# Cross attention: the maximum's scores in three units of one PSUM bank, and projections between the second and third pair of turned scores, in two banks

## What is computed

```python
q_c = _ln(x) @ W_qc + b_qc
kv_c = _ln(context) @ W_kvc + b_kvc
k_c, v_c = jnp.split(kv_c, 2, axis=-1)
...
c_attn_w = jax.nn.softmax(jnp.einsum('bhqd,bhsd->bhqs', q_c, k_c) * scale, axis=-1)
c_attn_out = jnp.einsum('bhqs,bhsd->bhqd', c_attn_w, v_c)
```

## Time and profile before

| | us |
|---|---|
| median of 3 runs (2774.58 to 2776.41) | 2776.03 |
| span of the profiled execution | 2771.8 |
| self-attention, about | 780 |
| cross-attention, about | 1230 |
| of it, one full body in the steady part | 74.45 |

### The profile page before, as it was taken

One profiled execution on the slowest core, in us unless ns is written; L12 is line 12 of the kernel. 1 busy time (PEld: TensorE's weight loads), 2 busy tenths in 40 slices (PEclk: granted clock), 3 DMA queues, 4 the chain that ended last, 5 costly groups with the idle time before them and its releaser, 6 DMA issues. The chain is left out here.

```text
span 2771.8 us, 50094 instructions
## 1 busy us (share of the span) xinstructions
PE 2667.6 (96%) x18676; PEld 2153.0 (78%) x18676; DVE 1743.5 (63%) x3285; ACT 1118.3 (40%) x2187; POOL 1296.9 (47%) x1447
## 2 busy tenths in 40 slices
PE   8999999999789999999999999999889999999997
PEld 6788888887677778777877877777568888888886
DVE  6777777777636777777777766776754444444431
ACT  4344444444434555555545555554532212112110
POOL 2344545444414676776676676666811220220211
PEclk9999999999899999999999999999789999999999
DMA  8454453545252443444344434433431111111110
GB/s 225 125 129 122 124 138 106 130 121 144 91 136 77 110 110 105 106 109 115 105 108 117 108 103 117 109 80 96 126 110 39 36 52 35 42 46 35 42 42 23
DMA packets 169359, 269.86 MB, mean 97 GB/s; under 512 B 28928, under 2 KB 83200, under 8 KB 169104
## 3 DMA queue, kind: packets, MB, share of 16 engines
q1 hardware_dynamic: 166048, 259.33, 34.5%
q0 software_dynamic: 3072, 7.34, 0.8%
HBM read 111.11 MB, written 36.77 MB: 53 GB/s over the span
## 5 line engine op out<-in xcount | busy, mean ns | idle before, releaser
L1490 DVE TENSOR_REDUCE cross_nmax<-cross_sc_ps 112x1 f32<-112x750 f32 x512 | 459.6, 928 | 162.7 <-PE cross_sc_ps L1365 162.6
L1608 ACT ACTIVATE cross_prT<-cross_tr_ps 125x448 f32<-125x448 f32 x768 | 389.9, 544 | 153.5 <-PE cross_tr_ps L1384 146.2
L1655 POOL TENSOR_TENSOR cross_part<-cross_prT 125x448 f32<-125x448 f32 x252 | 290.9, 1154 | 149.4 <-PE cross_or_ps L1404 83.4
L1017 POOL TENSOR_TENSOR self_psum<-self_prT 112x224 f32<-112x224 f32 x256 | 173.3, 677 | 349.4 <-ACT self_prT L907 337.0
L1384 PE MATMUL cross_tr_ps<-cross_qst,cross_kst 98*125 98x224 f32 x1536 | 314.4, 291 | 8.5 <-ACT cross_prT L1608 3.9
L1384 PEld LDWEIGHTS cross_tr_ps<-cross_qst,cross_kst 98*125 98x125 f32 x1536 | 244.6, 190 | 92.8 <-ACT cross_prT L1608 39.2
L1657 POOL TENSOR_TENSOR cross_part<-cross_part,cross_prT 125x448 f32<-125x448 f32 x252 | 291.9, 1158 | 19.8
L2052 ACT ACTIVATE mlp_hv<-mlp_h_ps,mlp_b 128x512 f32<-128x512 f32 x112 | 77.1, 689 | 519.8 <-PE mlp_h_ps L73 505.7
L1365 PE MATMUL cross_sc_ps<-cross_kst,cross_qst 96*112 96x500 f32 (+1 forms) x1024 | 274.2, 350 | 5.5 <-DVE cross_nmax L1490 2.3
L1969 DVE CAST mlp_hT_h<-mlp_hv 128x512 fp32r<-128x512 f32 x112 | 53.5, 477 | 319.1 <-ACT mlp_hv L2052 319.1
L907 ACT ACTIVATE self_prT<-self_st_ps 112x448 f32<-112x448 f32 x256 | 139.1, 544 | 210.6 <-PE self_st_ps L487 210.5
(11 more groups left out here) (247 smaller groups left out, 6644.9 us busy)
## 6 DMA issues: line engine op xcount, KB each, us to landing
cross_kst<-cross_nat_h SPq DMA_DIRECT2D x512, 93.8 KB, 2.2
cross_c_in<-in_context SPq DMA_DIRECT2D x96, 250.0 KB
cross_kst<-cross_nat_l SPq DMA_DIRECT2D x256, 93.8 KB, 2.2
cross_qst<-qc SPq DMA_DIRECT2D x192, 112.0 KB, 2.4
self_kst<-self_nat_h SPq DMA_DIRECT2D x128, 112.0 KB, 2.3
self_qst<-self_natq_h SPq DMA_DIRECT2D x128, 112.0 KB, 3.1
self_x_in<-in_x SPq DMA_DIRECT2D x16, 448.0 KB, 3.8
self_kst<-self_nat_l SPq DMA_DIRECT2D x64, 112.0 KB, 2.3
```

Source lines behind the costliest of these rows:

```text
L1017: pool.tensor_tensor(psum[:, j], prT[:, j, 0], prT[:, j, 1], ALU.add).then_inc(p_summed, 1)
L1490: dve.tensor_reduce(nmax[:, g % 2, t, j:j + 1], sc_ps[t][0:QN, SC0:SC0 + S], AX_X, ALU.max, negate=True).then_inc(maxed, 1)
L1608: act.activation(prT[:, slot(h), 2 * c:2 * c + 2], bank((h + LAG) % NH, c)[0:SN, 0:2 * N].rearrange("p (k t) -> p k t", k=2), ACT.Exp).the ...
L1655: pool.tensor_tensor(part[:], prT[:, j, 0:2], prT[:, j, 2:4], ALU.add).then_inc(pre_summed, 1)
```

## The change

The maximum's scores go into three units of one bank each (`UNITS`): 500 keys of the first half of the queries, 500 of the second, and the last 250 keys of both. Three reductions write `parts`, and one more instruction on DVE takes the smaller of the two negated maxima (`m_least`). Fills use two banks in turn, `even_ps` and `odd_ps`, by their place in `ORDER`, c tiles included, so the two banks `tr_ps` serve the turned scores alone. The maxima of four heads are turned in one transpose of 16 columns into `even_ps` or `odd_ps`, copied once and stored by two DMAs. The fill now stands between the second and the third pair of turned scores. `FILL` has its steps without a projection at 6 and 15, and step 15 has two c tiles.

```diff
-        sc_ps = [ps(f"sc_ps{i}", (P, 1024)) for i in range(QT)]
+        sc_ps = [ps(f"sc_ps{u}") for u in range(3)]
+        even_ps = ps("even_ps")
...
-        pj_ps = ps("pj_ps")
+        odd_ps = ps("odd_ps")
...
+        UNITS = (((0, 0, SHALF[0], 0),), ((1, 0, SHALF[0], 0),), ((0, SHALF[0], SHALF[1], 0), (1, SHALF[0], SHALF[1], SHALF[1])))
...
-        FILL = [[("k", 0, 0)], [("k", 0, 1)], [("k", 1, 0)], [("k", 1, 1)], [], [("k", 2, 0)], [("k", 2, 1)], [], [("v", 0)], [("k", 3, 0)], [("k", 3, 1), ("c", 0)], [("v", 1), ("c", 1)], [("v", 2), ("c", 2)], [("v", 3), ("c", 3)], [("v", 4), ("c", 4)], [("v", 5), ("c", 5)]]
+        FILL = [[("k", 0, 0)], [("k", 0, 1)], [("k", 1, 0)], [("k", 1, 1)], [("k", 2, 0)], [("k", 2, 1)], [], [("v", 0)],
+                [("k", 3, 0)], [("v", 1)], [("k", 3, 1)], [("v", 2), ("c", 0)], [("v", 3), ("c", 1)], [("v", 4), ("c", 2)],
+                [("v", 5), ("c", 3)], [("c", 4), ("c", 5)]]
...
+        TURN_BANK = (0, 1, 1, 0)
...
+        def bank_free(b, fill):
+
+            i = ORDER.index(fill)
+            return latest(b, i % 2, i)
...
         def bank(h, c):
-            return tr_ps[(3 * h + c + sum(len(tile_at(i)) for i in range(h))) % 2]
+            return tr_ps[(h + c) % 2]
...
-            def fill_(body_b, fill):
+            def fill_(body_b, fill, halves=(0, 1)):
...
+                if 0 in halves and body_b.c >= 0:
                     wait(pe, *bank_free(body_b, fill))
+                    wait(pe, m_row, body_b.n(KC, turns_before(fill)))
...
-            def score(b, h, t):
+            def score(b, h, u):
...
-                wait(pe, maxed, b.n(NH * QT, h * QT + t - 1))
+                wait(pe, maxed, b.n(NH * 3, h * 3 + u - 2))
...
-                wait(pe, exped, b.n(3 * NH, 3 * h + (1 if c == 2 else 0 if before or c == 1 else -1)))
+                wait(pe, exped, b.n(3 * NH, 3 * h + c - 1))
...
             def body(b, att, nxt, prv):
                 a = b.plus(1)
                 for h in range(NH):
-                    for c in range(ST // 2):
-                        for f, o in fill_at(b, h, "kv") if c == 1 else ():
-                            fill_(o, f)
...
+                    for o, l in late(b, h, att, prv):
+                        score_t(o, l, 0)
+                    for o, l in late(b, h, att, prv):
+                        score_t(o, l, 1)
+                    if h < NH - 1 and att:
+                        score(b, h + 1, 0)
...
+                    for f, o in fill_at(b, h, "kv"):
+                        fill_(o, f)
+                    if h % HPG == HPG - 1 and att:
+                        turn_maxima(b, h // HPG)
+                    for o, l in late(b, h, att, prv):
+                        score_t(o, l, 2)
+                    for u in (1, 2):
+                        if h < NH - 1 and att:
+                            score(b, h + 1, u)
...
             def split_maxima(b, g):
+                dve.wait_ge(maxed, b.n(NH * 3, 3 * HPG * (g + 1)))
+                dve.tensor_tensor(nmax[:, g % 2], parts[:, g % 2, 0], parts[:, g % 2, 1], ALU.min).then_inc(m_least, 1)
+                dve.wait_ge(m_least, b.n(KC, g + 1))
...
@@ block.scalar, body
-                        for f, o in fill_at(b, h, "kv") if c == 1 else ():
+                        for f, o in fill_at(b, h, "kv") if c == 2 else ():
                             high(o, f)
```

More of the change, by code:

```diff
@@ L1170, in fill_at, with evicted, latest, turns_before @@
             return [(f, b) for f in FILL[h] if f[0] in kinds and exists(b, f[0])]
[L1172 to L1177, removed]
+        def evicted(b, fill):
+            kind, *where = fill
+            o = b.plus(OF[kind])
             if kind == "k":
                 return k_l, o.n(2 * KC, 2 * where[0] + where[1] + 1)
-            return v_done, o.n(ST, where[0] + 1)
+            return {"v": v_done, "c": cT_l}[kind], o.n(ST, where[0] + 1)
+        TURN_BANK = (0, 1, 1, 0)
+        def latest(b, parity, count):
+            mine = [(b.plus(-1), f) for f in ORDER[parity::2] if b.c > 0 and exists(b.plus(-1), f[0])]
+            mine += [(b, f) for f in ORDER[:count][parity::2] if exists(b, f[0])]
+            return evicted(*mine[-1]) if mine else (v_done, ST)
+        def bank_free(b, fill):
+            i = ORDER.index(fill)
+            return latest(b, i % 2, i)
+        def turns_before(fill):
+            step = [h for h in range(NH) if fill in FILL[h]][0]
+            return (step + 1) // HPG if fill[0] == "c" else step // HPG
+        def turn_bank_free(b, g):
+            step = HPG * g + HPG - 1
+            return latest(b, TURN_BANK[g], sum(len(FILL[h]) for h in range(step)) + len([f for f in FILL[step] if f[0] != "c"]))
         def place(b, fill):
-            return pj_ps if b.c >= 0 else FIRST_BANKS[FIRST.index(fill) % len(FIRST_BANKS)]
-        def turn_bank(b, t):
-            return tr_ps[t % 2] if b.c < -1 else tr_ps[1]
+            if b.c >= 0:
+                return (even_ps, odd_ps)[ORDER.index(fill) % 2]
+            return tr_ps[fill[1] % 2] if fill[0] == "c" else FIRST_BANKS[FIRST.index(fill) % len(FIRST_BANKS)]
         def first_free(i):
@@ L1360, in score @@
                 if b.c == 0 and h == 0:
                     pe.wait_ge(v_done, ST)
-                if j == 1:
-                    wait(pe, m_row, b.n(QT * KC, QT * (g - 1) + t + 1))
-                for c0, cn in HALVES:
-                    last = pe.matmul(sc_ps[t][0:QN, SC0 + c0:SC0 + c0 + cn], qst[0:TERMS * HD, g, j, t * QN:(t + 1) * QN],
+                for t, c0, cn, at in UNITS[u]:
+                    last = pe.matmul(sc_ps[u][0:QN, at:at + cn], qst[0:TERMS * HD, g, j, t * QN:(t + 1) * QN],
@@ L1445, in _ @@
                     fill_(Batch(-1), ("c", t))
-            for t in range(QT):
-                score(Batch(0), 0, t)
+            for u in range(3):
+                score(Batch(0), 0, u)
             bodies(pe, body)
@@ L1538, in body @@
                         normalize(o, g)
-                    if h % HPG == HPG - 2 and att:
-                        split_maxima(b, h // HPG)
                     if due(b, h, 6) is not None:
@@ L1563, in _ @@
                     low(Batch(-1), ("c", t))
-            for t in range(QT):
-                row_max(Batch(0), 0, t)
+            for u in range(3):
+                row_max(Batch(0), 0, u)
             bodies(dve, body)
```

134 lines of the change are left out of this document (63 added, 71 removed).

## The result

| | before | after |
|---|---|---|
| median, 12 runs each | 2777.03 us (2774.58 to 2779.56) | 2782.68 us (2780.11 to 2783.78) |
| span of the profiled execution | | 2781.8 us |
| a steady body | 74.45 | 75.63 |

The ratio is 1.0019, 95% interval 1.0011 to 1.0028: 5.65 us or 0.2% slower. The two profiled executions lie 10.0 us apart, more than the medians do. I read where time goes from them, and its worth from the medians. The interval leaves out no change, if only just: 0.11% to 0.28%, or 3 to 8 us.

The account below looks back on a forecast made before the run. PE was taken as the bound, so only its stalls could move: 4.3 us added less 3.8 removed a body, taken as +0.6; 15 bodies give +9, the last +2, so 2787 us, 0.4% slower, range 2757 to 2803.

Parts of the forecast that it names:

- Step border: Between steps, pair 1 of turned scores waits for an exponential behind the fill's eviction: 0.47 us in six steps, 2.8 a body.
- Step 15: Behind c tile 3, pair 2 comes due before its exponential ends: stall 0.55, exposed 0.1, so 0.6 us added a body.
- step 0: The first fill waits for c tile 4's bank until DVE takes the low part: 0.55 us added a body.
- Step 6: In this step without a projection, scores meet a late DVE: 0.35 us added a body, bounds 0 and 0.6.
- Removed 3.8: Stalls the change removes a body: step borders 1.4, c-tile borders 0.6, steps 4, 6 and 7 1.4, turns of maxima 0.4.
- empty steps 4 and 7: Steps without a fill in the old table, stalls claimed to go: 0.6 us in step 4, 0.4 in step 7.
- DVE's third reduction: Extra maxima reduction, 2.5 us of DVE work a body, hidden while PE has a fill; only the body without fills pays.
- Fills' bank: Waits for the single projection bank: step 6's 0.4 us a body goes; by the skill's rule alone 4.3 to 6 overall.
- the last body, +2: In the body without fills DVE is the bound, so its third reduction costs 2.5 us at most, taken as 2.
- rival 1: Stalls inside go and borders cost no more than today: faster, 2754, half-way about 2760; chance 0.24.
- Rival 2: Added and removed stalls cancel, within 5.5 us of no change: 2776; chance 0.17.
- Rival 3: DVE becomes the bound as lateness of steps 4 to 6 carries on: 2810 to 2817 us; chance 0.06.

Follow-up runs that it names:

- e1: Changed kernel with ACT evicting a fill of keys or values behind its step's third exponential instead of ahead of it: 2765.31 us, ratio 0.9962.
- e9: Changed kernel with the maximum's first unit (one matmul of 500 columns) between pair 0 and pair 1 of the turned scores on PE: 2768.92 us.
- e10: Changed kernel with the edits of e1, e2, e3 and e9 together: 2738.83 us, ratio 0.9862.
- e3: Changed kernel with context tiles one step earlier, tiles 0 to 4 in steps 10 to 14 and tile 5 alone in step 15: 2774.67 us.
- e2: Changed kernel with DVE's inversion and normalisation directly behind the first maximum of their step instead of behind the low part: 2774.30 us.
- e5: Changed kernel with the fill table of before (steps 4 and 7 without a fill, one context tile each in steps 10 to 15): 2770.73 us.
- e12: Changed kernel with DVE's low part of a fill of keys ahead of its step's three maxima again: 2831.97 us, ratio 1.0199.
- e7: e3 with all key and value projections in one bank, context tiles and turned maxima in the other: 2835.62 us, ratio 1.0216.

## Why the prediction was right, and where its sizes were off

The sign and the main term held: a body's stalls grow because pair 1 waits behind the eviction, and the removed ones don't pay for it. 2787 was forecast, 2782.68 measured. That the total came so close is in part luck, as the end of the list shows. Term by term:

- **Step border, 0.47 six times**: right. Pair 1 starts 1.43 us after the last product (1.44 to 1.52 forecast), with the exponential as releaser. e1 and e9 show both halves of the mechanism, ACT's order and the lack of work on PE ahead of pair 1; in e10 the term is zero.
- **Step 15, 0.6, and step 0, 0.55**: right, 0.59 and 0.46 of wait and up to 0.1 behind them; e3 removes step 0's.
- **Step 6, 0.35 with bounds to 0.6**: mis-sized, it is 0.70 by distances between starts, and 0.75 a body is what e2 gives back. I had DVE's lateness, but let it meet the scores only, and not the bank that the values share with the normalisation. e2 shows it; it is more than half of why a body grew by 1.18 and not by 0.6.
- **Removed 3.8**: e5 puts the rest of the change, with the old table, at 0.19 us a body below the kernel before (74.26 against 74.45), and the table at +1.37. In my sum the empty steps 4 and 7 were worth 1.0 when gone; with two banks and three units they cost 0.45 and 0.35, under the 0.55 and 0.6 of steps 0 and 15 that the new table brings. Step 7, put at 0.4 by step 4's kind, lost about 0.23 in the kernel before: its turn and two pairs stand at 0.58 and 0.31 us where a step with a fill has 0.44 and 0.22.
- **DVE's third reduction, nothing in a full body**: it took 667 and 669 ns as forecast, and PE's scores wait for it in few places (5.6 us in 7 waits). That holds for the order of the change. It rests on the maxima standing first: with the low part ahead of them the kernel needs 49 us more (e12). That run moves the order and not the number of reductions, so how much of it is the third one's stays open.
- **Fills' bank, up to 0.4 a body**: right for this comparison, since the wait before was 4.3 us. But that row is not the second bank's worth in the new order. On the rule of the Trainium skill ("Perfetto Trace Analysis", Matmuls) that groups should rotate through different PSUM banks, e7 sides with the rule: without the rotation and with DVE's late low part the same kernel needs 61 us more.
- **Not in the sum**: body 0. I costed 15 bodies alike, but body 0 is 7.8 us shorter, and e5 puts 6.9 of that down to the table, whose fill in step 4 I had counted in a steady body only. And **the last body, +2**: from step 3 of body 14 to the last sums the changed kernel gains 0.4; DVE is busy 49.09 of 56 us there now, yet the work falls no further behind.

So the two profiles show +15.1 in 13 bodies where I had 13 x 0.6 = 7.8, and +1.2 behind the last sums where I had nothing. On the other side they show 9.5 us less than I had: -5.9 up to the third sums where +0.6 stood, -0.4 at the end where +2.6 stood (body 14 and the last one). The total of the profiles, +10.0 for a forecast of +11, came that close because these errors lean against each other. The medians moved by 5.65, half of the forecast.

The bounds that the prediction names for its forecast do not come out of its terms: the border at 0.44 to 0.52 six times and step 6 at 0 to 0.6 make 15 x -0.51 and 15 x +0.57, so 2779 to 2796 and not 2782 to 2798. Its half-way case of rival 1 would be 2765, not 2760.

Rival 1 fell as it stood, since ACT's order was what its own "against" said; e1 and e9 show that one edit each goes a third to a half of its 22 us (2765 and 2769). Rival 2, within 5.5 us of no change, is missed by next to nothing in time; what tells it from the forecast is the body, longer by 1.18 us where the rival has it as long as before. Rival 3 did not occur; e12 shows a kernel where DVE's order does bind, by another order than the rival's.

## What to carry to other kernels

Where two pairs of operations share two banks, the wait is set by the reader's order and by how much other work the writer has between them: put a short independent matmul between them, and evictions that nobody needs soon behind those that someone waits for (0.47 us, then 0.22, then nothing a border). A wait that a trace shows for a resource is its worth in that order only; when the order of its readers changes, measure the resource again. Time gained ahead of a later wait is swallowed there, so remove waits in order from the last one back. Cost the first and the last pass of a pipeline by themselves: there, work that hides a wait in a steady pass may be missing, and a table that costs 1.37 us in each steady body gave 6.9 us back in body 0.

## What was not expected of the hardware

A pair of turned scores or a product behind a wait cost about 0.1 us more until the next matmul started (0.32 instead of 0.22 for a pair, 0.28 instead of 0.172 for a product), after a wait of 0.12 us (e1's borders) as after one of 1.4 (e7's body 0). So the wait of 0.12 us that e1 leaves at a border costs 0.22. In the first body of the kernel before, the granted clock was 0.65 to 0.67 in stretches of 5 us behind PE's waits, and a product of 376 columns took 313 ns there (12 from 837.95 to 841.72) instead of 172. Two PSUM banks did not prevent it: e5 has the same 313 ns and 0.87 over the first 40 us.
